# A transformer decoder layer in one kernel: 256-token batches woven into the feed-forward loop

## The reference

```python
x = x + linear_attention(layernorm(x))      # 16 heads of 16: q, k = elu(.)+1, kv = k^T v, out = q kv / (q sum(k) + eps), o_w, o_b
x = x + softmax(mask((ctx Wq + bq)(ctx Wk + bk)^T / 8 * layernorm(x)))   # 256 x 256 per batch, ctx is 64 wide
h = fwht(layernorm(x) * SU_ug) / 64
h = silu(h @ W_gate.T * s_gate) * (h @ W_up.T * s_up)          # 1024 wide
x = x + fwht(h * SU_dp) / 64 @ W_down.T * s_down
```

## Time and profile before

| | us |
|---|---|
| median of 3 runs | 157.07 (156.5 to 158.38) |
| profiled execution, its span | 158.7 |
| PE busy in it | 132.9 (84%) |
| DVE busy | 103.1 (65%) |
| POOL busy | 72.5 (46%) |
| ACT busy | 66.0 (42%) |

### The profile page before, as it was taken

The page is one execution under the profiler, slowest core; times in us unless marked ns, Lnnn a source line. Parts: engine busy times, 40 slices in busy tenths (PEclk is TensorE's granted clock), DMA queues, the critical chain, the costliest instruction groups (busy, mean ns, idle before and its releaser), DMA issues.

```text
span 158.7 us, 1826 instructions
## 1 busy us (share of the span) xinstructions
PE 132.9 (84%) x605; PEld 106.4 (67%) x605; DVE 103.1 (65%) x204; ACT 66.0 (42%) x125; POOL 72.5 (46%) x62
## 2 busy tenths in 40 slices
PE   6859970089999995294599999997999999999992
PEld 2256750059978874183588888786888888888882
DVE  0655799998497899999739999966531124111142
ACT  0334400059466839122319668633744533223310
POOL 2316999980901397929200493284333213333300
PEclk9965998555999999959779999999999999999999
DMA  3999720000003100000400000000000003000003
GB/s 95 249 384 322 217 86 0 0 0 2 0 4 94 38 2 0 0 0 3 134 0 0 0 2 4 0 2 0 0 0 0 4 0 132 0 0 0 4 0 132
DMA packets 4103, 7.58 MB, mean 48 GB/s; under 512 B 509, under 2 KB 1597, under 8 KB 3966
## 3 DMA queue, kind: packets, MB, share of 16 engines
q1 hardware_dynamic: 3376, 6.69, 13.0%
q10 hardware_dynamic: 718, 0.78, 1.7%
HBM read 6.42 MB, written 1.05 MB: 47 GB/s over the span
## 4 chain that ended last, share of the span: by engine, by line
PE 50%; DVE 31%; issue 7%; ACT 4%; DMA 3%; POOL 2%; SPq 0%; DVEq 0%; POOLq 0%; ACTq 0%
PE bank L958 15%; PE bank L965 11%; DVE xn L544 9%; PE bank L849 5%; DVE x_res L674 4%; PE bank L914 4%; DVE st L533 4%; PE bank L863 4%; DVE score L653 3%; DMA x_res<-in_x 3%; PE bank L946 2%; PE bank L884 2%; ACT score L440 2%; PE bank L833 2%; PE bank L872 2%
## 5 line engine op out<-in xcount | busy, mean ns | idle before, releaser
L958 PE MATMUL bank<-xh,wug 128*128 128x512 f32 x192 | 45.9, 390 | 0.0
L958 PEld LDWEIGHTS bank<-xh,wug 128*128 128x128 f32 x192 | 35.7, 188 | 7.5 <-ACT eq L512 0.2
L334 POOL TENSOR_TENSOR dpre<-eq,dpre 128x512 fp32r<-128x512 f32 x15 | 20.1, 1341 | 43.9 <-ACT dpre L519 43.9
L785 DVE SCALAR_TENSOR_TENSOR eq<-bank,vecs,eq 128x512 f32<-128x512 f32 x16 | 11.9, 745 | 27.6 <-PE bank L958 26.4
L965 PE MATMUL bank<-dpre,wdh 128*128 128x512 f32 (+1 forms) x120 | 24.5, 349 | 0.0
L965 PEld LDWEIGHTS bank<-dpre,wdh 128*128 128x128 f32 x120 | 19.7, 189 | 3.1
L544 DVE TENSOR_SCALAR xn<-x_res,mv,rstd 128x256 f32<-128x256 f32 x16 | 19.8, 1291 | 2.2 <-POOL rstd L259 2.2
L849 PE MATMUL bank<-cst,xn 128*128 128x128 f32 x32 | 6.6, 374 | 16.2 <-DVE xn L544 16.2
L519 ACT CAST dpre<-eq 128x512 fp32r<-128x512 f32 x16 | 9.9, 620 | 20.9 <-DVE eq L785 20.9
L849 PEld LDWEIGHTS bank<-cst,xn 128*128 128x128 f32 x32 | 5.2, 192 | 17.8 <-DVE xn L544 15.0
L512 ACT ACTIVATE eq<-bank,vecs 128x512 f32<-128x512 f32 x16 | 11.0, 686 | 13.4 <-PE bank L958 10.1
(11 more groups left out here) (93 smaller groups left out, 220.1 us busy)
## 6 DMA issues: line engine op xcount, KB each, us to landing
stage<-in_w_ug SPq DMA_DIRECT2D x4, 512.0 KB, 4.3
wd_raw<-in_w_d SPq DMA_DIRECT2D x1, 1024.0 KB, 11.1
out<-score SPq DMA_DIRECT2D x3, 256.0 KB, 2.3
x_res<-in_x SPq DMA_DIRECT2D x2, 256.0 KB, 4.5
stage<-in_w_qkv SPq DMA_DIRECT2D x1, 512.0 KB, 8.4
x_res<-in_x SPq DMA_DIRECT2D x1, 512.0 KB, 9.3
rows<-in_row SPq DMA_DIRECT2D x1, 384.0 KB, 11.4
ctxT<-in_ctx_t ACTq DMA_DIRECT2D x1, 260.0 KB
```

What stands on the lines that cost most here:

```text
L334: g.tensor_tensor(hsp[:, 1, n % HR, :], sg[:, n % 2, :], hsp[:, 0, n % HR, :].bitcast(F32), ALU.subtract).then_inc(s["h_lo"], 1)
L785: v.scalar_tensor_tensor(sg[:, n % 2, :], B("up", h, j)[:, :], vecs[:, V_WSUG + j:V_WSUG + j + 1], sg[:, n % 2, :], ALU.mult, ALU.mult).th ...
L958: ins = mm(dst[:, :], wug[:, a, k, at + j * P:at + (j + 1) * P], xh[:, b, h, k, :], start=(i == 0), stop=(i == len(PASSES) - 1))
```

## The change

The whole kernel is rewritten in batches of 256 tokens (two tiles); the mathematics stays.

- **Shapes.** Every split product on activations now moves 256 columns instead of 512. Q of a batch is one bank (two blocks of 256), K is one bank, V is one bank; before, K and V of a tile shared one.
- **Biases** of Q, K and V: a matrix `bias_r` of 128 rows, zero except for three, times `ones`, is one more product at the end of each accumulation. The three rows are prepared by ACT (`bias_hi`) and GpSimd (`bias_parts`: one multiplication and one addition over 3 x 768). The PSUM value is then k + bias + 1, and ELU + 1 is one operation, max(min(exp(value - 1), 1), value), reading PSUM (`elu_k`, `elu_q`).
- **Masks**: added as bytes on GpSimd (two operations on int32 views), and converted with the factor in one operation over 2048 elements (`mask_bias`). Before, ACT converted both and GpSimd added.
- **Down product**: tokens on the output partitions. The hidden block is the stationary operand, `wdh` the moving one with 256 columns; all 8 blocks of a batch's hidden activations are kept (`hs`), and the down products of a batch run after its eighth `gate_up` step, 48 products. No transposes of x (`x2_turn`); results are added to `x_res` per tile and stored in token order, 8 stores of 128 KB.
- **Scales**: the down weight scale is multiplied into the weights on VectorE (`scale_pre`, two operations over 1024 elements), the signs into the Hadamard matrices and into the up scale (`sc_up`).
- **Order**: `HEAD` has batches 0 and 1 of attention, and batch 0 to `XH`. `SIDE` weaves the rest: batch 1's T3 and XH, all of batch 2, and the down weights' products into the steps of feed-forward batch 0; the end of batch 2's and all of batch 3's attention into that of batch 1; T3 and XH of batch 3 into that of batch 2. Group names: T1, T3 transposes after norm 1 and 3; K, V, Q; ST state; NUM numerator; AT transposed attention; OUT; SC scores; XH Hadamard; WD down weights; GU gate and up; Y result. The banks are dealt out in turn, group n gets bank n % 8.
- **Engines**: `ug_lo` and `h_lo` are all on GpSimd; layer norm 1 of batches 2 and 3 is normalised on ACT (`normalise1`); the staging buffers of the first half of the up and gate weights are later `xn3` and `sg`, the others were `ctxT` and `ux`; `pre` lies in the memory of `xh` of batches 2 and 3 and holds half of the down weights at a time, so `pre_hi(1)` waits for WD 1.
- **Start**: three products on zeros after the first product instead of seven; x in three loads (2, 2, 4 tiles), the weights of K, V and Q in three.

The core of the diff (in order: the two lists, GpSimd's sequence, three helpers, VectorE's sequence from the end of the head into feed-forward batch 0 and in batch 2, the down product, and TensorE's loop):

```diff
-HALVES = 2
-HT = TILES // HALVES
-HTOK = TOK // HALVES
-LAG = 3
+HEAD = (("mx", 0), ("u", 0), ("T1", 0), ("u", 1), ("SC", 0), ("K", 0), ("V", 0), ("Q", 0), ("ST", 0),
+        ("T1", 1), ("NUM", 0), ("K", 1), ("AT", 0), ("SC", 1), ("OUT", 0), ("V", 1), ("Q", 1), ("ST", 1),
+        ("SC", 2), ("NUM", 1), ("SC", 3), ("AT", 1), ("T3", 0), ("OUT", 1), ("XH", 0))
+SIDE = {(0, 0): (("T1", 2),), (0, 1): (("K", 2), ("V", 2), ("Q", 2)), (0, 2): (("T3", 1),), (0, 3): (("XH", 1),),
+        (0, 4): (), (0, 5): (("WD", 0), ("WD", 1), ("ST", 2)), (0, 6): (("WD", 2), ("WD", 3)),
+        (1, 0): (("NUM", 2),), (1, 1): (("T1", 3), ("AT", 2)), (1, 2): (("OUT", 2), ("K", 3), ("V", 3), ("Q", 3)),
+        (1, 3): (("ST", 3),), (1, 4): (("NUM", 3),), (1, 5): (("T3", 2), ("AT", 3)), (1, 6): (("XH", 2), ("OUT", 3)),
+        (2, 4): (("T3", 3),), (2, 5): (("XH", 3),)}
...
+            rstd_of(1, 0)
+            bias_parts()
+            rstd_of(1, 1)
+            mask_bias()
+            add_ob(0)
...
+            add_ob(1)
+            butterfly(0)
+            butterfly(1)
+            rstd_of(2, 0)
+            butterfly(2)
+            rstd_of(3, 0)
+            ug_lo(0)
             ug_lo(1)
+            rstd_of(1, 2)
+            shift_of(2)
+            add_ob(2)
+            rstd_of(2, 1)
             ug_lo(2)
+            h_lo(0)
+            ug_lo(3)
+            h_lo(1)
+            rstd_of(3, 1)
...
+            def bias_parts():
+                pool.wait_ge(s["bias_hi"], 1)
+                g.tensor_scalar(bias_r[0:3, :], bias_r[0:3, :].bitcast(F32), bias_raw[:, 3 * HID:3 * HID + 1], 1.0,
+                                ALU.mult, ALU.mult).then_inc(s["bias_mul"], 1)
+                pool.wait_ge(s["bias_mul"], 1)
+                pool.wait_ge(ld["bias_add"], 16)
+                g.tensor_tensor(bias_r[0:3, :], bias_r[0:3, :].bitcast(F32), bias_add, ALU.add)\
+                    .then_inc(s["bias"], 1)
...
+            def pre_hi(n):
+                part = slice(n * JB // 2, (n + 1) * JB // 2)
+                act.wait_ge(s["pre_scaled"], n + 1)
+                if n:
+                    wait_full(act, "WD", 1)
+                a.copy(pre[:, 0, :, :], wd_b[:, part, :]).then_inc(s["pre_hi"], 1)
...
+            def elu_k(b):
+                dve.wait_ge(s["ek"], b + 1)
+                if b >= 2:
+                    wait_full(dve, "ST", b - 2)
+                v.scalar_tensor_tensor(kp[:, b % 2, :, :].rearrange("p i d -> p (i d)"), ek[:, :], 1.0, B("K", b)[:, :],
+                                       ALU.min, ALU.max).then_inc(read_of("K", b), 1)
...
+            normalise(3, 0, xn3)
+            ln1_stats(2)
+            x3_lo(0)
             add_attn(1)
+            xh_lo(0)
+            ln_stats(2, 1)
+            xT_lo(2)
+            hidden(0)
             times_score(1)
             logits(1)
+            hidden(1)
+            elu_k(2)
+            softmax(1)
+            ln_stats(3, 1)
+            elu_q(2)
+            normalise(3, 1, xn3)
...
+            for n in range(2 * JB, 3 * JB):
+                hidden(n)
+                if n == 2 * JB:
+                    add_attn(3)
+                    ln_stats(2, 3)
+                    times_score(3)
+                    add_y(1)
+                    logits(3)
+                if n == 2 * JB + 2:
+                    softmax(3)
+                    ln_stats(3, 3)
+                if n == 2 * JB + 3:
+                    normalise(3, 3, xn3)
+                if n == 2 * JB + 4:
+                    x3_lo(3)
...
+            def down(b):
+                dst = [take("Y", b, i) for i in range(ST)]
...
+                def block_products(i, j):
+                    for n, (wa, hb) in enumerate(((1, 0), (0, 0), (0, 1))):
+                        ins = mm(dst[i][:, 0:HID], hs[:, hb, j, i * P:(i + 1) * P], wdh[:, wa, j, :],
+                                 start=(j == 0 and n == 0), stop=(j == JB - 1 and n == 2))
+                    return ins
...
+            for name, i in HEAD:
+                steps[name](i)
+            for b in range(BATCH):
                 for j in range(JB):
+                    gate_up(b, j)
+                    for name, i in SIDE.get((b, j), ()):
+                        steps[name](i)
+                down(b)
```

More of the change, by code:

```diff
@@ L17 @@
 HD = 16
+HPB = P // HD
 INTER = 1024
@@ new lines, in read_of, with wait_read @@
+        def read_of(name, i, t=0):
+            return read[bank_of[name, i, t]]
+        def wait_read(eng, name, i, t=0):
+            eng.wait_ge(read[bank_of[name, i, t]], turn_of[name, i, t] + 1)
+        loads = "x0 x1 x2 ident cst wk wv wq ctx wx bias bias_add vec row mss mkey wo wd ug0 ug1 ug2 ug3".split()
+        ld = {n: sem("ld_" + n) for n in loads}
+        st_out = [sem(f"st_out{t}") for t in range(TILES)]
+        names = ("fills junk bias_fill "
+                 "stats1 aggr1 eps1 rstd1 xn1 xn1s nmr stats2 aggr2 eps2 rstd2 stats3 aggr3 eps3 rstd3 xn3 "
+                 "w_hi w_lo bias_hi bias_mul bias msum mbias xb had_ready sc_up "
+                 "ug_hi ug_lo fly pre_scaled pre_hi pre_lo wd_hi "
+                 "xT_hi ek eq z_eps z_inv at "
```

1414 lines of the change are left out of this document (668 added, 746 removed).

## The result

| | before | after |
|---|---|---|
| median of the runs compared | 156.85 us | 181.13 us |
| ratio, 95% interval | | 1.147 [1.138, 1.156] |
| profiled execution, its span | 158.7 us | 180.4 us |

The change costs 24.3 us. The forecast was 174.2 us, slower, with a range of 159 to 188. The ratio goes by runs in the faster of two states alone; the profiled execution of the kernel after is the slowest of its four (182.38 us), and the spans of the other three are 176.9, 179.0 and 179.7 us.

The account below looks back on a forecast made before the run. It took the kernel as an 84 us latency-bound front, then 72 us bound by TensorE. Front 54, work 97.2, waits 20.2, clock 1.5 and tail 2.9 gave a 175.8 us span, 174.2 us as median; range 159 to 188.

Parts of the forecast that it names:

- T0: Start of the first gate-and-up product, ending the front: forecast at 54 us, bounds 47 and 60.
- The width of the products: Split products on TensorE: 256 columns cost 0.12 us each, so halving the width costs 6% more.
- Rival C: TensorE's narrow products: weight loads bind at 188 ns, adding 46 us, 220 in all; chance 0.02.
- the 129 us in the prediction: Time 684 halved products would need on TensorE at 188 ns per weight load, instead of 82 us.
- TensorE's work: TensorE's products and transposes left after the first gate-and-up product, at full clock: 97.2 us.
- The waits: TensorE idle after the front, before T3 1, WD 2 and down products, NUM 3, T3 3: 20.2 us, bounds 8 and 32.
- Half clock: Time TensorE loses to a lower granted clock after long idle time: 1.5 us, charged once.
- The mask's conversion: GpSimd's 2048-column operation in the front: 3.5 us taken, between 2.1 and 4.8.
- the step from span to median: Conversion of profiled span to median time: median 1.6 us below the span.
- A: Rival: chains just fit, front ends at 50 us, waits after it 8 us; span 158.1 us; chance 0.10.
- B: Rival: TensorE never kept waiting after the front; span 154.1 us; chance 0.08.
- D: Rival: GpSimd's port lock spreads to VectorE in feed-forward batch 0, 12 us more; span 188 us; chance 0.10.

Follow-up runs that it names:

- fill: Kernel after, with TensorE given extra 512-column products, later overwritten, in its four long waits: 177.72 us, ratio 1.133.
- before_narrow: Kernel before, with each 512-column gate-and-up product cut into two of 256: 158.25 us against 157.18, ratio 1.010.
- num3_early: Kernel after, with only diagonal(3) moved ahead of batch 2's softmax and statistics on VectorE: 181.77 us, ratio 1.157.
- woven6: Kernel after, with chains of batches 1, 2 and 3 moved earlier, separate memory for the scaled down weights, and front reordered: 158.62 us, ratio 1.002.
- woven7: woven6 with GpSimd's butterflies and ug_lo made to wait for VectorE's batch 0 and 1 operations, some operations reordered: 156.09 us, ratio 0.991.

## Why the prediction was right, step by step

**The verdict and its mechanism held.** The loss is where the sum put it: in waits at T3 1, WD, NUM 3 and T3 3. Shortening or removing three of them one at a time (T3 3, T3 1, WD 2) gave 8.7, 6.5 and 2.9 us, moving NUM 3's whole chain 3.0, and doing it all together with the reordered front brought the time back to that of before. The span came out 4.6 us above the sum: the slow clock was 3.9 too low, T0 2.4, and work and waits together 1.8 too high.

**T0: 54 forecast, 56.45 measured.** The chain is the one forecast. Four of its pieces in the chain of waits of the kernel after:

```profile
34.80 2.59 DVE score L684
37.40 2.47 DVE score L684
...
43.68 2.33 POOL wug L284
46.11 2.67 DVE front L610 x2
```

The two read-outs of the scores alternate with butterfly 2 (39.8 us, forecast 39.7), the normalisation waits for `ug_lo(0)`, and its second half for `ug_lo(1)`: 48.8 us, forecast 48.9. The Trainium skill ("SBUF — State Buffer", SBUF: two separate sides) says that two kinds of VectorE operation, those in a two-port performance mode and those with two SBUF inputs (the latter only against GpSimd operations that read SBUF), share a pair of ports with GpSimd, and that whichever starts first holds it for its whole instruction. The trace agrees: a read-out, with two SBUF inputs, takes 0.47 us alone and 2.5 to 2.6 beside a butterfly, while `elu_k`, with one input from SBUF and one from PSUM, takes 0.69 beside one (29.38 us, within the butterfly instruction from 29.13). The normalisations read one tensor from SBUF and were blocked too; the first kind would cover them, but no run shows in which mode they ran. What failed is the last piece, from T3 0 to T0: 7.6 us instead of 5.1. OUT 1 took 3.1 us and XH 0 2.2 where both were priced at full clock, and the windows from 48 to 54 us have a granted clock of 0.50. *fill*, which leaves the front alone, has the same there. So in this execution the front's error too is the clock's.

The 54 us were better, and the agreement at 48.9 more of an accident, than this one trace shows. Over the seven traces with the same front T3 0 starts at 46.5 to 48.9 us, 6.2 to 7.7 us pass from there to T0, and T0 lies from 52.68 to 56.59, in the middle at 54.95.

**The width of the products** held: 0.120 us each in the source view of L1014 from 160.0 us on:

```profile
L1014 PEld LDWEIGHTS bank<-xh_home,wug x96: 192/192/192, 159.9 to 171.3; 128*128 128x128 f32 x96
L1014 PE MATMUL bank<-xh_home,wug x96: 283/283/283, 160.0 to 171.4; 128*128 128x256 f32 x96
```

96 starts within 11.4 us, the same 283 ns of latency as in the earlier trace rows. Rival C fell in this trace and in *before_narrow*. The Trainium skill ("Trainium Kernel Development and Optimization", Best Practices) names two measures, the arithmetic done as a share of the peak and the busy share of weight loads. It doesn't say that loads come one after another; the 129 us in the prediction were my reading of it. By that reading these 96 loads would need 18.4 us, and the measurement decides against it.

**TensorE's work: 97.2 forecast, 95.9 measured.** The transposes were priced too high: four take 0.36 to 0.44 us, and I had read 0.87, which in the earlier trace rows is the time of twice as many; that is 3 us too much over seven groups. The text ahead of the prediction says that the trace shows a transpose as two instructions; it shows one (x4 for the four of T3 1), and two only for the small attention products. By the same misreading the 16 transposes of x2T that went were worth 1.7 us, not 3.5. Gate and up were priced about 1 too low (47.0 in *fill* against 46.1): a step between other groups takes 1.51 instead of 1.44.

**The waits: 20.2 forecast, 19.7 measured.**

| place | forecast | measured |
|---|---|---|
| T3 1 | 6.0 | 5.92 |
| WD 2, down products | 2.6 + 1.8 | 2.25 + 0.48 |
| NUM 3 | 3.5 | 3.23 |
| T3 3 | 6.3 | 7.16 |
| others | 0 | 0.64 |

That the sums agree to 0.5 us is partly luck, since the parts are off by up to 1.3. T3 3 is off by only 0.9 us because two errors partly cancel. Five steps run ahead of it, 7.4 us (the line of 60 products above), where I counted four and 5.8; and the chain takes 14.5 us from the first of them instead of 12.1. The down products did not wait 1.8 us for the last `wd_lo`: the step ahead of them ran at half clock and hid it (in *fill*, at full clock, 1.09 us of it show, ended by `wdh`), and the 0.48 us are a wait for the last hidden block. And the wait at NUM 3 is not NUM 3's alone: T3 2 behind it waits for the same stretch of VectorE's program, as *num3_early* showed.

**Half clock: 1.5 forecast, 5.4 measured.** This is the mis-sized term. I had the row for it, 1.7 us lost after one idle stretch, and charged it once: I counted two waits longer than that idle time of 3.0 us, though my 3.5 at NUM 3 was longer too, and let the next wait swallow the loss of the first. It does not. All four long waits of the profiled execution are followed by 1.3 to 1.5 us of loss: from T3 1 to XH 1, TensorE took 3.19 us in the kernel after and 1.92 in *fill*; from T3 3 to XH 3, 3.34 and 1.92; from WD 2 to the end of the next step and from NUM 3 to T3 2, 3.99 and 3.83 in the kernel after against 2.48 and 2.43. Only the first of the four is followed by another long wait, that of WD 2, and this one does not get shorter by it: 2.25 us, filled or idle, in *fill* too, where GU 3 ran at full clock, and in all eight traces that have the wait. By the program its chain starts at WD 1, a product of TensorE's own (`pre_hi(1)` waits for it), so what delays TensorE ahead of WD 1 delays both ends alike.

**Smaller sizes.** The mask's conversion took 1.90 us, under my lower bound of 2.1, which I had from a memset of another type. The two bias operations took 0.90 and 2.13 us, 3.0 together against 3.2. And the step from span to median was wrong in sign: the median lies 0.7 us above the profiled span, where I had set it 1.6 below, as with the kernel before. In every run on record the time is at least 1.7 us longer than the span of the same execution; before's median of 157.07 lay under its profiled span of 158.7, so the profiled execution was a longer one than those of the median. These 2.3 us are as large as the front's whole error.

**The rivals.** A needed waits of 8 us in sum and B none, and there were 19.7. D had the lock take 12 us more in batch 0 after T0; there it took 2.1 us at one read-out of the scores (at 63.11 us, 2.61 long, beside `ug_lo(3)`), 0.5 at the other and 0.5 at `pre_lo(0)`. It became real in *woven6*, where the butterflies were moved to that place.

**What stays open:** why T0 of one and the same front differs by 4 us between executions; why a wait of 2.25 us is followed by half clock in five traces and not in three; how much the biases cost; and whether woven7's 1% could be made more with GpSimd's butterflies (14 us), `ug_lo` (10 us) and hidden splits spread otherwise. Taking part of them to another engine wasn't tried.

## What to carry to other kernels

When work is woven into a loop that keeps the bounding engine busy, don't compare loads: follow each woven chain through the in-order programs of the other engines, from the step that starts it to the product that needs it, and compare its length with the steps in between. Put a chain whole ahead of the loop's own work on the helper engines, not one operation of it, and check what GpSimd runs beside each VectorE operation that takes all its tensors from SBUF: here the score operations with two and the normalisations with one were blocked, those reading PSUM were not. Charge every long wait of TensorE with the slow work that follows it, here 1.2 to 2.3 us after waits of 5.9 us and more in every trace, and in most, not all, after 2.3 and 3.2 too. Read more than one execution before calling a difference of 2 us an effect.
